# Sums of an attention kernel in runs of three half tiles, with one more buffer of probabilities and one fewer of rounded biases

## The reference

```
x = x + proj(attention(group_norm(x)))
# attention, for each image and each of 12 heads of 16 channels:
qkv    = x @ qkv_w + qkv_b
scores = scale * q @ k.T                          # 2304 x 2304
scores += rel_h[query, key row] + rel_w[query, key column]   # q @ tables
out    = softmax(scores) @ v
```

## Time and profile before

| | |
|---|---|
| median of 3 runs | 6778.15 us (6776.11 to 6785.65) |
| the profiled execution, its own time | 6786.55 us |
| span of that execution, first to last instruction | 6784.8 us |
| PE busy | 6704.2 us, 99% |
| DVE busy | 5449.1 us, 80% |
| ACT busy | 4750.3 us, 70% |

### The profile page before, as it was taken

How to read it: one execution, slowest core, us unless ns; L and a number is a source line. 1 busy time by engine, 2 the same in 40 slices (tenths; PEclk the granted TensorE clock), 3 DMA queues, 4 the chain that set the end, 5 groups by cost and what they waited for, 6 DMA issues and landing times.

```text
span 6784.8 us, 139135 instructions
## 1 busy us (share of the span) xinstructions
PE 6704.2 (99%) x53504; PEld 4237.1 (62%) x53504; DVE 5449.1 (80%) x9974; ACT 4750.3 (70%) x10225; POOL 939.8 (14%) x967
## 2 busy tenths in 40 slices
PE   7999999999999999999999999999999999999998
PEld 5666666666666666666666666666666666666664
DVE  7887888778887788877888778887888878878883
ACT  3777776767767777677776767767677676767775
POOL 2111010211112110121111211102101121101110
PEclk8999999999999999999999999999999999999999
DMA  6776676767777677667676766767677676777673
GB/s 163 150 157 152 138 160 136 166 151 142 153 147 167 144 145 157 150 156 149 142 153 150 159 144 143 160 146 168 140 145 157 147 165 138 143 152 156 142 155 90
DMA packets 306306, 1013.71 MB, mean 149 GB/s; under 512 B 107440, under 2 KB 196976, under 8 KB 215920
## 3 DMA queue, kind: packets, MB, share of 16 engines
q1 hardware_dynamic: 305648, 1004.81, 69.2%
HBM read 745.26 MB, written 255.69 MB: 148 GB/s over the span
## 4 chain that ended last, share of the span: by engine, by line
PE 95%; DMA 2%; DVE 1%; issue 0%; ACT 0%; POOL 0%; SPq 0%; POOLq 0%; ACTq 0%; DVEq 0%
PE work L807 30%; PE work L880 27%; PE work L798 27%; PE work L826 6%; PE work L845 3%; DMA moving<-rel_scratch 2%; PE work L864 2%; PE work L853 1%; DVE mpart L685 1%; DVE xb L676 0%; ACT probs L562 0%; DMA qk_scratch<-back 0%; DMA back<-attention_scratch 0%; PE work L832 0%; POOL back L506 0%
## 5 line engine op out<-in xcount | busy, mean ns | idle before, releaser
L685 DVE TENSOR_REDUCE mpart<-work 128x1 f32<-128x512 f32 (+1 forms) x8640 | 5078.9, 631 | 1065.1 <-PE work L807 998.7
L562 ACT ACTIVATE probs<-work 128x512 f32<-128x512 f32 (+1 forms) x8640 | 4100.1, 564 | 852.9 <-PE work L798 838.8
L807 PE MATMUL work<-mkeys,hi 128*128 128x512 f32 (+1 forms) x8640 | 3399.1, 394 | 9.4 <-DVE mpart L685 7.2
L798 PE MATMUL work<-moving,keys 113*128 113x512 f32 (+1 forms) x8640 | 3312.8, 384 | 13.5 <-DMA moving<-rel_scratch 7.9
L807 PEld LDWEIGHTS work<-mkeys,hi 128*128 128x128 f32 x8640 | 1644.2, 190 | 606.1 <-DVE mpart L685 322.8
L880 PE MATMUL work<-probs,vall 128*17 128x288 f32 x27648 | 2013.8, 409 | 0.0
L798 PEld LDWEIGHTS work<-moving,keys 113*128 113x128 f32 x8640 | 1641.6, 190 | 396.6 <-ACT probs L562 74.7
L880 PEld LDWEIGHTS work<-probs,vall 128*17 128x17 f32 x27648 | 637.5, 96 | 847.8 <-ACT probs L562 361.8
L826 PEld LDWEIGHTS work<-image,tab 128*48 128x48 f32 x6912 | 401.6, 124 | 545.9 <-ACT probs L562 513.6
L491 POOL TENSOR_TENSOR full<-full,hi 128x384 f32<-128x384 f32 x576 | 584.6, 1018 | 933.2 <-DVE hi L723 933.2
L496 POOL TENSOR_TENSOR rden<-oraw,rden 128x576 f32<-128x576 f32 x96 | 137.2, 1429 | 3946.9 <-DMA rden<-inverse_scratch 3946.9
(11 more groups left out here) (43 smaller groups left out, 629.2 us busy)
## 6 DMA issues: line engine op xcount, KB each, us to landing
moving<-rel_scratch SPq DMA_DIRECT2D x1728, 144.0 KB
moving<-qk_scratch SPq DMA_DIRECT2D x288, 576.0 KB
rel_scratch<-hi SPq DMA_DIRECT2D x192, 432.0 KB, 5.9
rel_scratch<-full SPq DMA_DIRECT2D x192, 432.0 KB, 5.5
moving<-rel_scratch SPq DMA_DIRECT2D x288, 288.0 KB
image<-qk_scratch SPq DMA_DIRECT2D x384, 144.0 KB, 3.2
keys<-qk_scratch SPq DMA_DIRECT2D x192, 288.0 KB, 7.8
qk_scratch<-split_hi SPq DMA_DIRECT2D x144, 192.0 KB, 3.9
```

Of the source, the lines that this page charges most:

```text
L562: act.activation(probs[:, tile % RING, lo:up], bank[:, 0:up - lo], ACT.Exp).then_inc(act_read, 1)
L685: dve.tensor_reduce(mpart[:, u % 2, q, m:m + 1], bank[:, 0:MSPLIT[m][1] - MSPLIT[m][0]], AX.X, ALU.max)\
L798: pe.matmul(bank[:, 0:up - lo], tile_of(keys[0:K_ROWS, u % 2, :], c, third), moving[0:K_ROWS, slot_of(u, third)[0], lo:up], start=True, st ...
L807: pe.matmul(bank[:, 0:up - lo], hi[:, u % 2, q * P:(q + 1) * P], mkeys[:, u % 2, lo:up], start=True, stop=True).then_inc(for_dve, 1)
```

## The change

A run of sums now has three half tiles (12 matmuls, 24 entries in the trace) instead of two (8 and 16). There are two runs in three tiles instead of three: one before place 3 of tiles 2, 5, 8, 11, 14 and 17, and one at place 5 of tiles 0, 3, 6, 9, 12 and 15, with the second half of the tile before the last and the whole last tile. For that the probabilities get a third buffer (`RING = 3`). The 9 KB per partition come from `hi`, which has one buffer instead of two. So that the last block of `hi` is not rounded while the matmuls of the running unit still read it, `high` of that block moves from place 2 of tile 13 to place 0 of tile 14, and the first block of a unit waits for the store of the unit just before. The numbers computed are the same.

```
--- before.py
+++ after.py
@@ -30,7 +30,7 @@
 QT = N // P
 MAXB = 5
 QCOL = N // 8
-RING = 2
+RING = 3
 BANKS = 3
 K_ROWS = 113
 TBW = 2 * SIDE
@@ -40,6 +40,7 @@
 SB = len(SPLIT)
 MSPLIT = SPLIT[-1:] + SPLIT[:-1]
 MT_AT = 2
+EARLY = 3
 
 QK_AT = 1
 SLOTS = 5
@@ -138,7 +139,7 @@
         probs = sb("probs", [P, RING, N])
         moving = sb("moving", [P, SLOTS, N], F32R)
         keys = sb("keys", [P, 2, N], F32R)
-        hi = sb("hi", [P, 2, N], F32R)
+        hi = sb("hi", [P, N], F32R)
         mkeys = sb("mkeys", [P, 2, N], F32R)
         full = sb("full", [P, N])
         image = sb("image", [P, N], F32R)
@@ -451,7 +452,7 @@
                         image_load(u + 3)
                     if t == 13 and u + 2 < UNITS:
                         sp.wait_ge(hi_ready, NB * (u + 3))
-                        rel_store(u + 2, hi[:, (u + 2) % 2, :].bitcast(F32), 0, rel_hi_stored)
+                        rel_store(u + 2, hi[:, :].bitcast(F32), 0, rel_hi_stored)
                     if t == 14 and 0 <= u + 1 < UNITS:
                         top_load(u + 1, 0)
                     if t == 14 and u + 2 < UNITS:
@@ -488,7 +489,7 @@
             def low(u, r):
                 cols = slice(r * BLK, (r + 1) * BLK)
                 pool.wait_ge(hi_ready, NB * u + r + 1)
-                pool.tensor_tensor(full[:, cols], full[:, cols], hi[:, u % 2, cols].bitcast(F32), ALU.subtract)\
+                pool.tensor_tensor(full[:, cols], full[:, cols], hi[:, cols].bitcast(F32), ALU.subtract)\
                     .then_inc(lo_ready, 1)
 
             def normalise(u):
@@ -718,9 +719,9 @@
                 dve.wait_ge(act_read, place["rel", u, 7 + r // 2 * 2] + 1)
                 if r == 0:
                     dve.wait_ge(fullq_in, 32 * (u + 1))
-                    if u >= 2:
-                        dve.wait_ge(rel_hi_stored, 32 * (u - 1))
-                dve.tensor_copy(hi[:, u % 2, cols], full[:, cols]).then_inc(hi_ready, 1)
+                    if u >= 1:
+                        dve.wait_ge(rel_hi_stored, 32 * u)
+                dve.tensor_copy(hi[:, cols], full[:, cols]).then_inc(hi_ready, 1)
 
             def top(u):
                 dve.wait_ge(dve_read, place["max", u, QT - 1, MAXB - 1] + 1)
@@ -752,8 +753,10 @@
                                 constants()
                         if u >= 1 and (t, i) == (4, 5) and u <= UNITS:
                             invert(u - 1)
-                        if 8 <= t < 14 and i == 2 and -2 <= u and u + 2 < UNITS:
+                        if 8 <= t < 13 and i == 2 and -2 <= u and u + 2 < UNITS:
                             high(u + 2, t - 8)
+                        if t == 14 and i == 0 and -2 <= u and u + 2 < UNITS:
+                            high(u + 2, NB - 1)
                         if (t, i) == (TILES - KEEP - 1, 5) and 0 <= u + 1 < UNITS and u >= -1:
                             top(u + 1)
                         if s + 1 < STAGES and j == 3:
@@ -804,7 +807,7 @@
                         pe.wait_ge(hi_ready, NB * u + q // 3 + 1)
                     if m == 0 and q == 0:
                         pe.wait_ge(mkeys_in[u % 2], 32 * (u // 2 + 1))
-                    pe.matmul(bank[:, 0:up - lo], hi[:, u % 2, q * P:(q + 1) * P], mkeys[:, u % 2, lo:up],
+                    pe.matmul(bank[:, 0:up - lo], hi[:, q * P:(q + 1) * P], mkeys[:, u % 2, lo:up],
                               start=True, stop=True).then_inc(for_dve, 1)
                 elif item[0] == "rel":
                     _, u, r = item
@@ -865,28 +868,34 @@
                                        start=(t == 0), stop=(t == 1))
                     mm.then_inc(for_dve, 1)
 
-            def attend(tile):
+            def attend(tile, part):
                 u, t = divmod(tile, TILES)
                 _, b, h = unit(u)
-                if t == 0:
+                if t == 0 and part == 0:
                     if h == 0:
                         pe.wait_ge(dve_read, place["v", u // HEADS, QT // 2 - 1] + 1)
                     if u:
                         pe.wait_ge(o_read, 2 * u)
                 pe.wait_ge(act_read, scored(tile))
-                for part in range(2):
-                    for j in range(4):
-                        at = (2 * j + part) * QCOL
-                        mm = pe.matmul(sums[32 * j:32 * j + VCOL, part, 0:QCOL], vall[:, b * QT + t, h, :],
-                                       probs[:, tile % RING, at:at + QCOL], start=(t == 0), stop=(t == TILES - 1))
-                mm.then_inc(attended, 1)
+                for j in range(4):
+                    at = (2 * j + part) * QCOL
+                    mm = pe.matmul(sums[32 * j:32 * j + VCOL, part, 0:QCOL], vall[:, b * QT + t, h, :],
+                                   probs[:, tile % RING, at:at + QCOL], start=(t == 0), stop=(t == TILES - 1))
+                if part == 1:
+                    mm.then_inc(attended, 1)
 
             for u in range(-3, UNITS + 2):
                 for t in range(TILES):
                     tile = TILES * u + t
                     for i in range(SB + 1):
-                        if i == SB and 0 < tile <= TILES * UNITS:
-                            attend(tile - 1)
+                        if i == EARLY and t % 3 == 2 and 0 <= u < UNITS:
+                            attend(tile - 2, 0)
+                            attend(tile - 2, 1)
+                            attend(tile - 1, 0)
+                        if i == SB and t % 3 == 0 and 0 < tile <= TILES * UNITS:
+                            attend(tile - 2, 1)
+                            attend(tile - 1, 0)
+                            attend(tile - 1, 1)
                         for item in plan[u][t][i]:
                             fill(item)
                         if 0 <= u < UNITS and i < SB:
```

## The result

The kernel with the change takes 7098.19 us (median of 4 runs, 7092.37 to 7101.49) against 6781.28 us of the kernel before, run beside it: a ratio of 1.0463 [1.0451, 1.0476], 317 us longer. The forecast was 7007, 229 longer. So the sign and the mechanism came out as argued, the size did not: the time lies 3 us above the upper end of the range, and 88 of the 317 us have to be explained.

What follows compares the result with a forecast made beforehand. PE, busy 99%, was taken as the bound. Per unit, 1.52 saved against 3.34 of new waits gave 175 us longer; with 29 for transfers and 25 for projection heads, 7016 profiled, 7007 us median, range 6880 to 7095.

Steps and rivals of the forecast that it cites:

- Transfers, in size: Rows for tile 11 arrive late because fewer runs lie between tiles 8 and 11: 0.3 a unit, 29 us longer.
- No drain at the tables: Tables behind a plain matmul start no later than a maximum would; nothing added. Rival with a drain: 7090 to 7180, chance 0.05.
- the banks hold: Rival: bank turns are really under 1.18, PE waits no more than today; about 6632, up to 6700 us; chance 0.09.
- half: Rival: the waits come out at half and about cancel the gain; 6778 us within 14; chance 0.03.
- Transfers set the pace: Rival: rows of tile 11 late by the whole 1.7 in each unit; 7141 us; chance 0.06.
- A wait of 0.16 at `mt` in tile 14 ... goes: At matmul `mt` in tile 14, an existing wait of 0.16 a unit disappears with the change.
- Restart of PE: 0.06.: At a PE matmul whose bank is released late, the weight load starts 0.06 after the release.
- Moved and freed at no cost.: The moved last cast of `hi`, its single buffer and the third probabilities buffer delay nothing; SP's next steps wait anyway.
- The saving of 1.52.: Fixed cost of runs per unit falls from 5.16 to 3.64 us: 1.52 saved, 146 us in 96 units.
- The walk of tiles 15 to 17: Bank waits at boundaries in these tiles, such as 0.12 + 0.25 + 0.13 = 0.50 from 16 to 17; 0.72 in all.
- Tile 2.: ACT's copies of finished sums in tile 1 make tile 2's table wait 0.58 and its next score 0.17: 0.75.
- Heads with projections.: In 7 of 12 heads, projection or value matmuls take ring places: 0.45 a unit in 56 units, 25 us longer.

Runs made afterwards that it cites:

- two pairs with small readers: Kernel before and changed kernel, maxima and exponentials on 64 columns only: 6718.45 and 6715.14 us; also without row loads for tiles 3 to 17: 6701.65 and 6609.73 us.
- the small pair: Kernel before and changed kernel, each with maxima and exponentials on the first 64 columns of each bank only: 6718.45 and 6715.14 us.
- early_0: Changed kernel with the early run moved from place 3 to place 0 of tiles 2, 5, ...: 6939.08 us.
- buffers_only: Changed kernel's buffers and moved cast, with the kernel before's run of two half tiles after every tile: 6806.75 us.
- the pairs without row loads: Kernel before and changed kernel without row loads for tiles 3 to 17: 6769.43 and 7061.22 us with full readers, 6701.65 and 6609.73 us with 64-column readers.
- mt_3: Changed kernel with the matmul `mt` of tile 14 at place 3 instead of place 2: 7066.90 us.
- bank_wait_last: Changed kernel with PE's two waits at a tile's first score swapped, so the bank's wait sits on the weight load: 7084.90 us.
- sums_out_first: Changed kernel with ACT copying both halves of the finished sums at place 0 of tile 1: 7071.71 us.
- the four mended places: Changed kernel with `mt` at place 3, sums copied out first, bank's wait last and the `hi` store at SP's tile 14, together: 7049.83 us.
- before_two: Kernel before with the sums copied out first in tile 1 and the 256-column score at place 0 instead of 4: 6799.78 us.

## Why the prediction was right in direction and too low

Right, and shown by runs:
- *That a run saves, and its length.* 1.31 to 1.33 in a plain unit by the two pairs with small readers, 1.65 for a run of 24 entries.
- *The waits outweigh it, because twelve boundaries have lost the run in which DVE and ACT emptied the banks.* With fast readers the loss is gone (the small pair), with six bare boundaries for twelve half of it is (`early_0`), and with the old runs nearly all of it (`buffers_only`). The boundary from tile 16 to 17 shows DVE's pace of 0.60.
- *Transfers, in size*: 25 us by the pairs without row loads, 29 forecast. The place was luck: of PE's 16.9 us of waits on rows, 2.5 stand at tile 11, which the forecast named; 4.3 stand at tile 9 and 10.1 at tile 14.
- *No drain at the tables*: 0.12.

Of the rivals, "the banks hold" and "half" fall by the same runs. "Transfers set the pace" is wrong for the change; a kernel with fast readers does meet the rows as its next limit, above all at tile 9.

Wrong, the size of the waits: 3.34 a unit on record. Measured, 2.83 + 1.31 = 4.14. The steps that failed:
- *"A wait of 0.16 at `mt` in tile 14 ... goes", and "`mt` gives DVE 0.11 back".* I followed the banks of that matmul and not its operand. Before, a run stood between the last maximum of tile 13 and `mt`, and DVE's reduction to `mcol` lay beside it. Without that run `mt` itself waits for `mcol`. Tiles 12 to 14 are 0.39 over, and `mt_3` gives back 35 us of the 88. This is the largest single piece that a run shows.
- *"Restart of PE: 0.06."* It was read from tile 1 and applied to every matmul. The first score of a tile has two waits, and restarts in 0.11 when the separate one is met last. `bank_wait_last` shows 0.26 a plain unit, 25 us, of which 15 show in the whole.
- *"Moved and freed at no cost."* The buffers cost 19 us. The sentence on SP looked at SP's next steps and not at the loads of the projection out behind them; some 8 of the 19 seem to lie there.
- *The saving of 1.52.* It came out at 1.31, 0.21 short, 20 us in 96 units. Which of its terms is too high, no run shows; the 0.12 in it was called not shown.
- *The walk of tiles 15 to 17* is 0.24 over by the starts of the matmuls (0.33 in the table). At 16 to 17 m0 waits 0.24 and not 0.12. And weights exposed by the last wait hold the stream: from m2's load to the start of the next score the trace has 0.34, not 0.23 (4408.37 to 4408.71). I had put this 0.10 into the turn of a bank, where it delays the reader, and not behind the last wait, where nothing is left to hide it. Over the trace 654 of 844 late loads of 512-column maxima (those that begin 0.03 to 0.07 after a maximum's end, after more than 0.1 of idle time) show the 0.34; no run tested it alone.
- *Tile 2.* The mechanism held (`sums_out_first`: 30 us), but tiles 0 to 2 are 0.21 over. Of that the restart is 0.10, as `bank_wait_last` has 11.72 there.
- *Tiles 9 to 11* came out 0.13 lower than forecast by the starts of the matmuls (0.24 in the table): the 0.18 for tile 11 and the 0.24 behind it seem too much together.
- *Heads with projections.* No row stood behind the 0.45 a unit, 25 us. By the traces their 56 units lengthen by 3.18 in the mean and 3.23 in the median, units of heads 9 to 11 by 3.05 and 2.89: 0.14 to 0.34 a unit, 8 to 19 us.

Added up, the plain unit is 272 - 175 = 97 us over: 20 from the saving, 77 from the waits. Of the 77, `mt` makes 35 and the restart 25; the other 17 go to the walk of the remaining places, above all tiles 15 to 17, less what tiles 9 to 11 gave. Outside of the plain unit 45 us stand where 54 was forecast, and 97 less 9 is the 88. Rows (25), buffers (19) and heads (8 to 19) come to more than that 45, so they overlap or are each a little too high; how, is open. Open stays also why the four mended places give 50 and not 101 us together (late loads are seen, but not shown to be all of it), 11 of the 19 us of the buffers, and why `before_two` is slower.

## What to carry to other kernels

Work on the bound engine that its readers don't have to read, such as a run of sums, is also the time in which these readers catch up. Before such runs are merged, compare the turn of a bank (matmul, reading, restart, exposed weights) with the time of as many places as the ring has banks, at each boundary that loses its run. For each matmul that loses its cover walk both its bank and its operand, and check what a faster stream would ask of the transfers.

## What the runs showed of the hardware

- Where a PE instruction of this kernel has two waits, one of them is an instruction of its own: a release of that one restarts PE after 0.11 us, a release of the one on the weight load after 0.05. The order in the code decides which is which (`bank_wait_last`).
- A 512-column matmul behind a late bank costs 0.10 us more than the wait: 0.34 from its weight load to the next matmul's start and not 0.23.
- A saving worth 92 us without the row loads can leave the kernel's time where it was (3 us), when transfers were only just in time before.
